# Byte offsets of TensorE's operands: g in rows of 2064 bytes, g_lo 8 bytes further, and h, p and a at multiples of 64

## The chip, the cores and the metric

One core of a Trainium2 chip runs the whole program. The metric is device time of one execution in microseconds. The clock of TensorE is told below as the granted clock of the trace, as a share of 2.4 GHz.

## What is computed

The input x has 32 images of 32 x 32 positions with 256 channels. Each image goes through a group normalisation, a one-head attention over its 1024 positions and an output projection, and x is added:

```python
h = group_norm(x)                      # 32 groups of 8 channels
q, k, v = h @ Wq + bq, h @ Wk + bk, h @ Wv + bv
attn = softmax((q @ k.T) * 256 ** -0.5)        # 1024 x 1024 for each image
out = x + (attn @ v) @ Wo + bo
```

## The kernel before

**Number format.** Every large product is made of three products in float32r: each factor is split into a rounded part (hi) and the rest (lo), and hi x hi, hi x lo and lo x hi are summed in PSUM.

**Folded weights.** At the start, Wq and Wk are folded into one matrix a, and Wv and Wo into one matrix vo, so that an image needs the projection g = a.h + g_bias, the scores g.h, the projection v = h.vo, and the attention p.v.

**Stages of TensorE.** The order is written out by hand. Each image b has five kinds of stage, and a matmul here is one instruction with its own weight load of 128 x 128:

- `project_g` (G): 24 matmuls with 512 columns each. Stationary is a, moving is h. The result goes through ScalarE (`g_part`, writes g_hi) and VectorE (`g_rest`, writes g_lo).
- `scores` (S): twice 48 matmuls with 512 columns, for the halves c = 0 and 1 of the queries. Stationary is h (columns m x 128), moving is g (block kk, c). For each m they come as (h_hi, g_hi), (h_hi, g_lo), (h_lo, g_hi) for kk = 0 and then for kk = 1.
- `project_v` (V): 48 matmuls with 256 columns. Stationary is h, moving is vo.
- `attend` (A): twice 96 matmuls with 258, 256 and 258 columns in turn. Stationary is p_hi or p_lo, moving is v_hi (rows of 258 columns) or v_lo (rows of 256).

The sequence for one image in the steady loop is `scores(b, 0)`, `attend(b - 1, 1)`, `project_v(b)`, `scores(b, 1)`, `attend(b, 0)`, `project_g(b + 1)`. Over 32 images this makes 768 G, 3072 S, 1536 V and 6144 A matmuls, 11520 in all. ScalarE and VectorE do the softmax and the splits beside it; SyncE and GpSimd issue the transfers.

**Where the tensors lie.** `sb(name, shape)` allocates a tensor in SBUF behind the one before it, at the next multiple of 32 bytes. So the order of the calls and their sizes set every start address. In the built program the tensors that TensorE reads start at these bytes of each partition:

| tensor | bytes before | past a multiple of 64 | bytes after | past a multiple of 64 |
|---|---|---|---|---|
| a_hi, a_lo | 17568, 19616 | 32 | 17536, 19584 | 0 |
| vo_hi, vo_lo | 21664, 23712 | 32 | 79200, 81248 | 32 |
| h_hi, h_lo | 35008, 43200 | 0 | 29824, 38016 | 0 |
| g_hi, g_lo | 51392, 59584 | 0 | 46208, 54464 | 0 (g_lo is read from 8 on) |
| v_hi, v_lo | 67776, 76032 | 0 | 62720, 70976 | 0 |
| p_hi (c = 0, 1) | 118368, 134752 | 32 | 83328, 99712 | 0 |
| p_lo (c = 0, 1) | 151136, 167520 | 32 | 116096, 132480 | 0 |

Inside the tensors, weight blocks and the blocks of h, p, a, vo and v_lo lie multiples of 512 bytes apart, so they keep the tensor's offset. A row of v_hi has 258 columns, 1032 bytes, so row m starts 8m bytes past a multiple of 64.

Of the kernel before, what the change touches and what calls it, by code (L numbers as in the profile page):

```python
# [31 lines left out]
F32 = mybir.dt.float32  # L32
F32R = mybir.dt.float32r
ALU = mybir.AluOpType
ACT = mybir.ActivationFunctionType
AX_X = mybir.AxisListType.X

P = 128
# [4 lines left out]
def attention_kernel(nc, x, x_turned, wq, bq, wk, bk, wv, bv, wo, bo, out):  # L43
    B, H, W, C = x.shape
    N = H * W
    T = N // P
    K = C // P
    CH = 2
    Q = N // CH
# [6 lines left out]
    NG = SQ // GC  # L56
    QB = Q // SQ
    SB = 4
    VC = C + 2
    SCALE = float(C) ** -0.5  # L60


# [3 lines left out]
    with ExitStack() as ctx:  # L66
        def sb(name, shape, dt=F32):
            return ctx.enter_context(nc.sbuf_tensor(name, shape, dt))
# [4 lines left out]
        def banks(name, n):  # L73
            return [ctx.enter_context(nc.psum_tensor(f"{name}{i}", [P, 512], F32)) for i in range(n)]
# [4 lines left out]
        ps_s = banks("ps_s", SB)  # L79
        ps_o = banks("ps_o", TQ)  # L80
        ps_g = [ps_o[0], ps_o[1], ps_s[2], ps_s[3]]
# [3 lines left out]

        ident = sb("ident", [P, P])
        ones = sb("ones", [P, P])
        minus_half = sb("minus_half", [P, NG])
        a_hi = sb("a_hi", [P, K, C], F32R)
        a_lo = sb("a_lo", [P, K, C], F32R)  # L90
        vo_hi = sb("vo_hi", [P, K, C], F32R)
        vo_lo = sb("vo_lo", [P, K, C], F32R)
        g_bias = sb("g_bias", [P, K])
        out_bias = sb("out_bias", [P, C])


        x_t = sb("x_t", [P, K, N])
        h_hi = sb("h_hi", [P, K, N], F32R)
        h_lo = sb("h_lo", [P, K, N], F32R)
        g_hi = sb("g_hi", [P, K, N], F32R)  # L100
        g_lo = sb("g_lo", [P, K, N], F32R)
        v_hi = sb("v_hi", [P, T, VC], F32R)
        v_lo = sb("v_lo", [P, T, C], F32R)
        bn_parts = sb("bn_parts", [P, K, 2, 6])


# [10 lines left out]


        s_buf = [sb(f"s_buf{c}", [P, T, Q]) for c in range(CH)]
        p_hi = [sb(f"p_hi{c}", [P, T, Q], F32R) for c in range(CH)]  # L120
        p_lo = [sb(f"p_lo{c}", [P, T, Q], F32R) for c in range(CH)]
        top2 = sb("top2", [P, 2, Q])
        top_turned = sb("top_turned", [P, Q])
        part_max = sb("part_max", [P, QB])
# [67 lines left out]
        def after(eng, semaphore, value):  # L192

            if not isinstance(value, int) or value > 0:
                eng.wait_ge(semaphore, value)
# [54 lines left out]
        def _(pool):  # L250
# [4 lines left out]
            pool.memset(v_hi[:, :, C:C + 1].bitcast(F32), 1.0).then_inc(const_step, 1)  # L255
            pool.memset(v_hi[:, :, C + 1:VC].bitcast(F32), 0.0).then_inc(const_step, 1)
            pool.wait_ge(const_step, 6)
# [28 lines left out]
        def _(act):  # L286
# [12 lines left out]
            def g_part(b, i):  # L299
                act.wait_ge(g_ps, b * 4 + (i + 1))  # L300
                c, k = i // 2, i % 2
                nc.scalar.activation(g_hi[:, k, c * Q:(c + 1) * Q], ps_g[i][:], ACT.Identity,
                                     bias=g_bias[:, k:k + 1]).then_inc(g_hi_done, 1)

            def v_part(b, i):
# [10 lines left out]
            def exponentials_hi(b, c, i):  # L316

                rows = slice(i * PIECE, (i + 1) * PIECE)
                if i == 0:
                    after(act, o_ps, b * 8 + (4 * c + 4 - 8))  # L320
                act.wait_ge(diff_done, b * 8 + (4 * c + i + 1))
                nc.scalar.activation(p_hi[c][:, rows, :], s_buf[c][:, rows, :], ACT.Exp,  # L322
                                     scale=SCALE).then_inc(p_hi_done, 1)

            def exponentials(b, c, i):

                piece = s_buf[c][:, i * PIECE:(i + 1) * PIECE, :]
                nc.scalar.activation(piece, piece, ACT.Exp, scale=SCALE).then_inc(p_done, 1)  # L328

# [20 lines left out]
            for i in range(4):  # L350
                g_part(0, i)
# [36 lines left out]
            def body(b, first, last):  # L388

                scores_out(b, 0, 0)  # L390
                if not first:
                    last_exponentials(b - 1, 1)
                for m in range(1, T):
                    scores_out(b, 0, m)
                if first:
                    first_softmax()
                else:
                    softmax_beside(b, 0, lambda i: v_part(b, i))
                    scores_out(b, 1, 0)
                    last_exponentials(b, 0)  # L400
                    for m in range(1, T):
                        scores_out(b, 1, m)
                if not last:
                    h_parts(b + 1)
                softmax_beside(b, 1, nothing if last else (lambda i: g_part(b + 1, i)))
# [6 lines left out]
        def _(dve):  # L412
# [69 lines left out]

            def g_rest(b, i):
                c, k = i // 2, i % 2
                cols = slice(c * Q, (c + 1) * Q)
                dve.wait_ge(g_hi_done, b * 4 + (i + 1))
                nc.vector.scalar_tensor_tensor(out=g_lo[:, k, cols], in0=ps_g[i][:], scalar=g_bias[:, k:k + 1],
                                               in1=g_hi[:, k, cols].bitcast(F32), op0=ALU.add,
                                               op1=ALU.subtract).then_inc(g_lo_done, 1)

            def v_rest(b, i):
# [100 lines left out]
            for i in range(4):  # L592
                g_rest(0, i)
# [59 lines left out]
            def body(b, first, last):  # L653
# [26 lines left out]
                if not first and not last:  # L680
                    normalise(b + 1)
                maxima(b, 1, 3)
                maxima(b, 1, 4)
                softmax_beside(b, 1, lambda j: finish(b, 0, j), nothing if last else (lambda k: h_rest(b + 1, k)),
                               nothing if last else (lambda i: g_rest(b + 1, i)), nothing, nothing)

            images(dve, body)
# [5 lines left out]
        def _(pe):  # L693
            def product(ps, pairs, sem_done, start=True, stop=True):

                for n, (stationary, moving) in enumerate(pairs):
                    last = nc.tensor.matmul(ps, stationary, moving, start=start and n == 0,  # L697
                                            stop=stop and n == len(pairs) - 1)
                if sem_done is not None:
                    last.then_inc(sem_done, 1)  # L700
# [54 lines left out]
            def scores(b, c, m):  # L755

                if m == 0:
                    pe.wait_ge(g_lo_done, b * 4 + (2 * c + 2))
                if m in (2, 3):

                    pe.wait_ge(v_lo_done if c else g_lo_done, b * 4 + (m + 1))
                after(pe, s_out, b * 16 + (8 * c + m + 1 - SB))
                rows, cols = slice(m * P, (m + 1) * P), slice(c * Q, (c + 1) * Q)
                product(ps_s[(8 * c + m) % SB][:], [(h[:, kk, rows], g[:, kk, cols]) for kk in range(K)
                                                    for h, g in ((h_hi, g_hi), (h_hi, g_lo), (h_lo, g_hi))], s_ps)

            def attend(b, c, j):
# [7 lines left out]
                for m in range(T):  # L775
                    if j == 0 and m % PIECE == 0:
                        pe.wait_ge(p_lo_done, b * 8 + (4 * c + m // PIECE + 1))
                    nc.tensor.matmul(ps[:, 0:VC], p_hi[c][:, m, cols], v_hi[:, m, :], start=m == 0, stop=False)  # L778
                    nc.tensor.matmul(ps[:, 0:C], p_hi[c][:, m, cols], v_lo[:, m, :], start=False, stop=False)  # L779
                    last = nc.tensor.matmul(ps[:, 0:VC], p_lo[c][:, m, cols], v_hi[:, m, :], start=False,  # L780
                                            stop=m == T - 1)
# [25 lines left out]
            def body(b, first, last):  # L807
                for m in range(T):
                    scores(b, 0, m)
                if not first:  # L810
                    for j in range(TQ):
                        attend(b - 1, 1, j)
                project_v(b)
                for m in range(T):
                    scores(b, 1, m)
                for j in range(TQ):
                    attend(b, 0, j)
                if not last:
                    project_g(b + 1)
# [35 lines left out]
```

## Time and profile before

| | us |
|---|---|
| median of 2 runs | 1836.41 (1836.28 to 1836.55) |
| the profiled execution | 1837.21 |
| its span, first to last instruction | 1835.5 |
| TensorE busy | 1815.1 |
| TensorE's weight loads busy | 1655.1 |
| VectorE busy | 1662.1 |
| ScalarE busy | 985.9 |
| mean granted TensorE clock | 0.994 |

The span is what the trace covers; the profiled execution has 1.7 us outside it. A matmul's busy time in the trace is longer than the distance from its start to the next one's start, since matmuls overlap in the array. So the distance of two starts, here called the pitch, is what a matmul costs on a TensorE that never rests, and the timeline is the view to read it from.

### The profile page before, as it was taken

What the parts mean: (1) busy time and instruction counts of PE and PEld (TensorE: products, weight loads), DVE (VectorE), ACT (ScalarE), POOL (GpSimd) and SP (SyncE); (2) the same over time, 40 slices, a digit from 0 to 9 for tenths busy, and PEclk for the clock granted to TensorE, in tenths of its full rate; (3) what the DMA queues carried; (4) which work ended last, traced back from release to release, by engine and by line L of the source; (5) the groups of instructions that cost most, each with busy time, mean ns of one, the idle gap of its engine ahead of it and who ended that gap; (6) DMA issues with size and microseconds to landing.
All of it is one profiled execution on the core that took longest, in us unless ns stands there. A gap on an engine that the chain in (4) does not pass through costs nothing.

```text
span 1835.5 us, 32744 instructions
## 1 busy us (share of the span) xinstructions
PE 1815.1 (99%) x11586; PEld 1655.1 (90%) x11586; DVE 1662.1 (91%) x2922; ACT 985.9 (54%) x1352; POOL 91.1 (5%) x107
## 2 busy tenths in 40 slices
PE   8999999999999999999999999999999999999997
PEld 7899999899898999998998989999989989899996
DVE  7899999999999999999999999999999999999985
ACT  4564654654645646546555456465465554564652
POOL 0000000000000000000000000000000000000000
PEclk9999999999999999999999999999999999999998
DMA  3221222221222212222212222122222122221211
GB/s 115 58 69 34 46 69 57 69 62 18 69 57 69 69 34 46 69 57 69 61 19 69 57 69 69 30 50 69 57 69 59 21 69 57 69 69 27 53 23 24
DMA packets 29296, 101.92 MB, mean 56 GB/s; under 512 B 3681, under 2 KB 4706, under 8 KB 29282
## 3 DMA queue, kind: packets, MB, share of 16 engines
q0 software_dynamic: 9216, 33.56, 11.6%
q1 hardware_dynamic: 20066, 68.17, 11.6%
q8 instruction: 9, 0.15, 0.0%
q14 instruction: 5, 0.04, 0.0%
HBM read 68.16 MB, written 67.11 MB: 74 GB/s over the span
## 4 chain that ended last, share of the span: by engine, by line
PE 98%; DVE 1%; DMA 0%; issue 0%; SPq 0%; POOLq 0%; ACT 0%; DVEq 0%
PE ps_s L697 48%; PE ps_o L778 13%; PE ps_o L780 13%; PE ps_o L779 13%; PE ps_o L697 10%; DMA s_buf<-in_L_conv_Wk_dram 0%; DVE p_lo L545 0%; DVE s_buf L537 0%; DVE v_lo L493 0%; PE ps_o L709 0%; DVE top L507 0%; DVE query_max L524 0%; PE ps_s L709 0%; POOLq L66 0%; SPq L213 0%
## 5 line engine op out<-in xcount | busy, mean ns | idle before, releaser
L778 PE MATMUL ps_o<-v_hi,p_hi 128*128 128x258 f32 x2048 | 580.3, 283 | 3.2 <-DVE p_lo L545 3.2
L780 PE MATMUL ps_o<-v_hi,p_lo 128*128 128x258 f32 x2048 | 580.6, 284 | 0.0
L779 PE MATMUL ps_o<-v_lo,p_hi 128*128 128x256 f32 x2048 | 578.1, 282 | 0.0
L322 ACT ACTIVATE p_hi<-s_buf 128x1024 fp32r<-128x1024 f32 x256 | 272.0, 1062 | 525.8 <-DVE s_buf L537 525.8
L697 PE MATMUL ps_s<-g_hi,h_hi 128*128 128x512 f32 x1024 | 398.6, 389 | 1.5 <-DVE v_lo L493 1.5
L697 PE MATMUL ps_s<-g_hi,h_lo 128*128 128x512 f32 x1024 | 399.5, 390 | 0.0
L697 PE MATMUL ps_s<-g_lo,h_hi 128*128 128x512 f32 x1024 | 398.9, 390 | 0.0
L778 PEld LDWEIGHTS ps_o<-v_hi,p_hi 128*128 128x128 f32 x2048 | 389.0, 190 | 6.1 <-issue 2.2
L779 PEld LDWEIGHTS ps_o<-v_lo,p_hi 128*128 128x128 f32 x2048 | 388.6, 190 | 3.0
L780 PEld LDWEIGHTS ps_o<-v_hi,p_lo 128*128 128x128 f32 x2048 | 388.5, 190 | 0.0
L314 ACT ACTIVATE s_buf<-ps_s 128x512 f32<-128x512 f32 x512 | 292.9, 606 | 167.9 <-PE ps_s L697 164.0
L545 DVE TENSOR_TENSOR p_lo<-s_buf,p_hi 128x1024 fp32r<-128x1024 f32 x256 | 306.6, 1218 | 32.0 <-ACT s_buf L328 32.0
L537 DVE TENSOR_TENSOR s_buf<-s_buf,row_max 128x1024 f32<-128x1024 f32 x256 | 306.6, 1218 | 1.1
L328 ACT ACTIVATE s_buf<-s_buf 128x1024 f32<-128x1024 f32 x256 | 270.9, 1058 | 0.0
L697 PEld LDWEIGHTS ps_s<-g_hi,h_hi 128*128 128x128 f32 x1024 | 192.4, 188 | 41.4 <-DVE v_lo L493 2.0
L697 PEld LDWEIGHTS ps_s<-g_hi,h_lo 128*128 128x128 f32 x1024 | 192.2, 188 | 40.2
L697 PEld LDWEIGHTS ps_s<-g_lo,h_hi 128*128 128x128 f32 x1024 | 192.2, 188 | 39.5
L507 DVE TENSOR_TENSOR top<-top,s_buf 128x512 f32<-128x512 f32 (+1 forms) x192 | 166.8, 869 | 46.9 <-ACT s_buf L314 35.6
L557 DVE SCALAR_TENSOR_TENSOR o_buf<-ps_o,rden,out_bias 128x256 f32<-128x256 f32 x256 | 123.9, 484 | 14.7
L265 POOL DMA_DIRECT2D out_dram<-o_buf x64 | 57.0, 891 | 1429.0 <-DVE o_buf L557 1358.9
L307 ACT ACTIVATE v_hi<-ps_o 128x512 fp32r<-128x512 f32 x64 | 38.3, 599 | 107.0 <-PE ps_o L697 107.0
L507 DVE TENSOR_TENSOR top<-s_buf 128x1024 f32<-128x1024 f32 x64 | 78.3, 1223 | 8.2 <-ACT s_buf L314 8.2
(89 smaller groups left out, 2202.9 us busy)
## 6 DMA issues: line engine op xcount, KB each, us to landing
x_t<-in_x_turned_dram SPq DMA_DIRECT2D x64, 512.0 KB, 3.7
out_dram<-in_x_dram SPq DMA_DIRECT2D x64, 512.0 KB, 7.5
out_dram<-o_buf POOLq DMA_DIRECT2D x64, 512.0 KB, 5.5
s_buf<-in_L_conv_Wq_dram SPq DMA_DIRECT2D x1, 256.0 KB, 5.0
s_buf<-in_L_conv_Wk_dram SPq DMA_DIRECT2D x1, 256.0 KB, 6.2
s_buf<-in_L_conv_Wv_dram SPq DMA_DIRECT2D x1, 256.0 KB, 5.5
s_buf<-in_L_conv_Wo_dram SPq DMA_DIRECT2D x1, 256.0 KB, 6.6
s_buf<-in_L_conv_bq_dram SPq DMA_DIRECT2D x1, 1.0 KB, 6.3
```

The lines of the kernel that those rows point to most:

```text
L265: pool.dma_start(out_v[b, :, c * TQ:(c + 1) * TQ, :], o_buf[c][:], accum_op=ALU.add).then_inc(stored[c], 16)
L314: nc.scalar.activation(s_buf[c][:, m, :], ps_s[(8 * c + m) % SB][:], ACT.Copy).then_inc(s_out, 1)
L322: nc.scalar.activation(p_hi[c][:, rows, :], s_buf[c][:, rows, :], ACT.Exp, scale=SCALE).then_inc(p_hi_done, 1)
L328: nc.scalar.activation(piece, piece, ACT.Exp, scale=SCALE).then_inc(p_done, 1)
L507: nc.vector.tensor_tensor(to, left, right, ALU.max).then_inc(top_step, 1)
L537: nc.vector.tensor_tensor(piece, piece, row_max[:].unsqueeze(1).broadcast_to([P, PIECE, Q]), ALU.subtract).then_inc(diff_done, 1)
L545: nc.vector.tensor_tensor(p_lo[c][:, rows, :], s_buf[c][:, rows, :], p_hi[c][:, rows, :].bitcast(F32), ALU.subtract).then_inc(p_lo_done, 1)
L557: nc.vector.scalar_tensor_tensor(out=o_buf[c][:, j, :], in0=ps_o[j][:, 0:C], scalar=rden[:, t:t + 1], in1=out_bias[:], op0=ALU.mult, op1=A ...
L697: last = nc.tensor.matmul(ps, stationary, moving, start=start and n == 0, stop=stop and n == len(pairs) - 1)
L778: nc.tensor.matmul(ps[:, 0:VC], p_hi[c][:, m, cols], v_hi[:, m, :], start=m == 0, stop=False)
L779: nc.tensor.matmul(ps[:, 0:C], p_hi[c][:, m, cols], v_lo[:, m, :], start=False, stop=False)
L780: last = nc.tensor.matmul(ps[:, 0:VC], p_lo[c][:, m, cols], v_hi[:, m, :], start=False, stop=m == T - 1)
```

## The change

The tensors are allocated in another order, and g gets a gap of 4 columns behind each block of 512. Of a block with index 2k + c, g_hi then starts 16 (2k + c) bytes past a multiple of 64: 0 and 32 for c = 0, 16 and 48 for c = 1. g_lo starts 8 bytes behind each: 8 and 40 for c = 0, 24 and 56 for c = 1. The small tensors `shift` and `shift_back` are never used; they put vo at 32 past a multiple of 64 and p at 0. Against their stationary operand (as "moving minus stationary", modulo 64) the moving operands stand like this:

| stage | before | after |
|---|---|---|
| G (h against a) | 32 | 0 |
| S (g against h) | 0 | 0, 8, 0, 32, 40, 32 for c = 0; 16, 24, 16, 48, 56, 48 for c = 1 |
| V (vo against h) | 32 | 32 |
| A (v_hi, v_lo, v_hi against p) | 8m + 32, 32, 8m + 32 | 8m, 0, 8m |

No instruction is added, removed or moved on any engine: each engine's list has the same instructions with the same shapes in the same order, and the waits are the same.

```diff
+    GROW = Q + 4
...
-        minus_half = sb("minus_half", [P, NG])
+
         a_hi = sb("a_hi", [P, K, C], F32R)
         a_lo = sb("a_lo", [P, K, C], F32R)
-        vo_hi = sb("vo_hi", [P, K, C], F32R)
-        vo_lo = sb("vo_lo", [P, K, C], F32R)
-        g_bias = sb("g_bias", [P, K])
-        out_bias = sb("out_bias", [P, C])
-
-
         x_t = sb("x_t", [P, K, N])
         h_hi = sb("h_hi", [P, K, N], F32R)
         h_lo = sb("h_lo", [P, K, N], F32R)
-        g_hi = sb("g_hi", [P, K, N], F32R)
-        g_lo = sb("g_lo", [P, K, N], F32R)
+
+        g_rows = [sb("g_hi", [P, K, CH, GROW], F32R), sb("g_lo", [P, K, CH, GROW], F32R)]
+        g_hi, g_lo = g_rows[0][:, :, :, 0:Q], g_rows[1][:, :, :, 2:2 + Q]
         v_hi = sb("v_hi", [P, T, VC], F32R)
         v_lo = sb("v_lo", [P, T, C], F32R)
+        sb("shift", [P, 8])
+        vo_hi = sb("vo_hi", [P, K, C], F32R)
+        vo_lo = sb("vo_lo", [P, K, C], F32R)
+        sb("shift_back", [P, 8])
+        p_hi = [sb(f"p_hi{c}", [P, T, Q], F32R) for c in range(CH)]
+        p_lo = [sb(f"p_lo{c}", [P, T, Q], F32R) for c in range(CH)]
+
+        minus_half = sb("minus_half", [P, NG])
+        g_bias = sb("g_bias", [P, K])
+        out_bias = sb("out_bias", [P, C])
...
-        p_hi = [sb(f"p_hi{c}", [P, T, Q], F32R) for c in range(CH)]
-        p_lo = [sb(f"p_lo{c}", [P, T, Q], F32R) for c in range(CH)]
...
-                product(ps_s[(8 * c + m) % SB][:], [(h[:, kk, rows], g[:, kk, cols]) for kk in range(K)
+                product(ps_s[(8 * c + m) % SB][:], [(h[:, kk, rows], g[:, kk, c, :]) for kk in range(K)
```

`g_part` and `g_rest` index g in the same new way.

## Rows read from the trace of the kernel before

**Rows 1.** The page: busy time of each engine, and the chain that ended last

```profile
PE 1815.1 (99%) x11586; PEld 1655.1 (90%) x11586; DVE 1662.1 (91%) x2922; ACT 985.9 (54%) x1352; POOL 91.1 (5%) x107
...
PE 98%; DVE 1%; DMA 0%; issue 0%; SPq 0%; POOLq 0%; ACT 0%; DVEq 0%
```

**Rows 2.** The waits of TensorE: us in total, times, longest

```profile
PE ps_o L778 <- DVE p_lo L545: 3.2, 2, 2.0
PE ps_o L697 <- issue: 2.1, 1, 2.1
PE ps_o L786 <- POOL ident L258: 2.0, 1, 2.0
PE ps_o L709 <- DMA s_buf<-in_L_conv_Wk_dram: 1.9, 1, 1.9
PE ps_s L697 <- DVE v_lo L493: 1.5, 1, 1.5
```

**Rows 3.** Timeline, TensorE, scores of image 3, c = 1: start, duration (us)

```profile
213.97 0.40 PE L697 MATMUL ps_s<-g_hi,h_hi 128*128 128x512 f32 x1
...
214.67 0.39 PE L697 MATMUL ps_s<-g_hi,h_hi 128*128 128x512 f32 x1
214.90 0.39 PE L697 MATMUL ps_s<-g_lo,h_hi 128*128 128x512 f32 x1
...
216.05 0.39 PE L697 MATMUL ps_s<-g_hi,h_hi 128*128 128x512 f32 x1
...
224.44 0.39 PE L697 MATMUL ps_s<-g_lo,h_hi 128*128 128x512 f32 x1
```

**Rows 4.** The same view, the next image's project_g and the start of its scores

```profile
236.42 0.40 PE L697 MATMUL ps_o<-h_hi,a_hi 128*128 128x512 f32 x1
...
239.21 0.40 PE L697 MATMUL ps_s<-h_hi,a_hi 128*128 128x512 f32 x1
...
242.01 0.39 PE L697 MATMUL ps_s<-g_hi,h_hi 128*128 128x512 f32 x1
```

**Rows 5.** The same view at project_g of image 1, behind a wait

```profile
66.41 0.47 PE L697 MATMUL ps_o<-h_hi,a_hi 128*128 128x512 f32 x1 [2.09 <-issue]
...
67.29 0.63 PE L697 MATMUL ps_o<-h_hi,a_hi 128*128 128x512 f32 x1
...
69.85 0.63 PE L697 MATMUL ps_o<-h_hi,a_hi 128*128 128x512 f32 x1
```

**Rows 6.** Stretches: us, busy by engine (instructions), granted clock, DMA share, GB/s

```profile
core 0: us, PE busy (x) PEld busy (x) DVE busy (x) ACT busy (x) POOL busy (x), PEclk, DMA share, GB/s
...
67.30:70.20 2.90, 2.90 (x8) 2.33 (x7) 2.87 (x5) 2.58 (x3) 0.00 (x0) 0.50 0.94 332
...
200.00:220.00 20.00, 20.00 (x146) 18.94 (x145) 18.43 (x35) 11.28 (x16) 0.86 (x1) 1.00 0.17 26
```

**Rows 7.** Timeline, TensorE: the first matmul of project_v of image 3

```profile
208.28 0.29 PE L697 MATMUL ps_o<-vo_hi,h_hi 128*128 128x256 f32 x1
```

**Rows 8.** Timeline, TensorE: first and last matmul of attend(3, 0)

```profile
224.90 0.28 PE L778 MATMUL ps_o<-v_hi,p_hi 128*128 128x258 f32 x1
...
236.29 0.28 PE L780 MATMUL ps_o<-v_hi,p_lo 128*128 128x258 f32 x1
```

More of the change, by code:

```diff
@@ L301, in g_part @@
                 c, k = i // 2, i % 2
-                nc.scalar.activation(g_hi[:, k, c * Q:(c + 1) * Q], ps_g[i][:], ACT.Identity,
+                nc.scalar.activation(g_hi[:, k, c, :], ps_g[i][:], ACT.Identity,
                                      bias=g_bias[:, k:k + 1]).then_inc(g_hi_done, 1)
@@ L484, in g_rest @@
                 c, k = i // 2, i % 2
-                cols = slice(c * Q, (c + 1) * Q)
                 dve.wait_ge(g_hi_done, b * 4 + (i + 1))
-                nc.vector.scalar_tensor_tensor(out=g_lo[:, k, cols], in0=ps_g[i][:], scalar=g_bias[:, k:k + 1],
-                                               in1=g_hi[:, k, cols].bitcast(F32), op0=ALU.add,
+                nc.vector.scalar_tensor_tensor(out=g_lo[:, k, c, :], in0=ps_g[i][:], scalar=g_bias[:, k:k + 1],
+                                               in1=g_hi[:, k, c, :].bitcast(F32), op0=ALU.add,
                                                op1=ALU.subtract).then_inc(g_lo_done, 1)
@@ L762, in scores @@
                 after(pe, s_out, b * 16 + (8 * c + m + 1 - SB))
-                rows, cols = slice(m * P, (m + 1) * P), slice(c * Q, (c + 1) * Q)
-                product(ps_s[(8 * c + m) % SB][:], [(h[:, kk, rows], g[:, kk, cols]) for kk in range(K)
+                rows = slice(m * P, (m + 1) * P)
+                product(ps_s[(8 * c + m) % SB][:], [(h[:, kk, rows], g[:, kk, c, :]) for kk in range(K)
                                                     for h, g in ((h_hi, g_hi), (h_hi, g_lo), (h_lo, g_hi))], s_ps)
```

## The prediction

> **What bounds the kernel now.** I read the page first, for which engine the end hangs on. TensorE is busy 1815.1 of 1835.5 us and makes 98% of the chain that ended last [rows 1]. Its waits for others sum to 10.7 us in six places [rows 2], so nothing but the pace of its own 11520 matmuls is left to shorten. VectorE is next with 1662.1 us [rows 1], 173 us below the span; in 20 us of the steady loop it is busy 18.43 us [rows 6]. A TensorE faster by a per cent or two would not run into it often.
>
> Then I read the pace in the timeline, by the pitch from one start to the next. In each stage I compare it with the bare columns at the granted clock of 1.00 [rows 6], which is 2.4 GHz: 512 columns take 213.3 ns, 256 take 106.7.
>
> - S, settled: from 216.05 to 224.44 there are 37 pitches, 8.39 us, 226.8 ns each: 13.4 over the columns [rows 3].
> - S, unsettled: after project_v the first nine pitches, 213.97 to 216.05, take 2.08 us, 231.1 each, and one of them (214.67 to 214.90) takes 0.23 [rows 3]. The same operands' offsets thus give two paces.
> - G: the last twelve pitches, 239.21 to 242.01, take 2.80 us, 233.3 each: 20.0 over the columns. The first twelve, 236.42 to 239.21, take 2.79 [rows 4].
> - V: 48 pitches from 208.28 to 213.97 take 5.69 us, 118.5 each: 11.9 over [rows 3, 7].
> - A: 96 pitches from 224.90 to 236.42 take 11.52 us, 120.0 each. Two in three have 258 columns, so the columns are 107.2 and the excess is 12.8 [rows 4, 8].
>
> The excess over the columns is 3072 x 13.5 + 768 x 20 + 1536 x 11.9 + 6144 x 12.8 ns = 41 + 15 + 18 + 79 = 153 us. That is all that any placement of operands can win.
>
> Two more things speak of where the excess comes from. Image 1's project_g runs at a granted clock of 0.50, 1.2 GHz [rows 6], behind a wait of 2.09 us; its pitch is then (69.85 - 67.29) / 6 = 426.7 ns, exactly 512 columns at 1.2 GHz [rows 5]. The excess is gone when the array asks for columns half as fast, so it is not a fixed cost of an instruction; it is the feeding of the operands. And G and S are the same shape, the same type and the same count of weights. What differs is that g lies at 0 against h (modulo 64 bytes), while h lies at 32 against a. G costs 6.5 ns more for each matmul. That is the only pair in this trace from which a price of the offset can be read, and it is a correlation in two stages.
>
> A rule of the Trainium skill speaks against any effect at all. SBUF — State Buffer, in the section on two separate sides, and TensorE: Matmul & The Clock Gate, in the steps of a matmul, say that TensorE has one read port for the moving operand and another for the weights, so that a load does not take bandwidth from a running matmul. By that rule the offsets change nothing. The second page's section on the back-to-back gap gives 512 columns 2.5 ns over the bare columns; this trace shows 13.4 and 20.0, so something that this rule leaves out is at work here.
>
> **The change part by part.** It moves no instruction, so each term is a count times a change of pitch. The 10.7 us of waits stay; they are before first results and at the last image.
>
> *a to offset 0 (G).* h against a goes from 32 to 0, what S has now. If the pitch goes from 233.3 to S's 226.8, 24 matmuls x 6.5 ns x 31 images (one has ten at the low clock) = 4.8 us. If each project_g first passes through nine unsettled pitches at 231.1, as S does behind project_v, 9 x 4.3 x 31 = 1.2 us of it are lost. The ends are 0 and -5; I take **-4 us**, nearer to the settled row, since scores behind project_g settle at once.
>
> *g spread over eight offsets (S).* This is the largest unknown: 3072 pitches, 3.1 us for each ns. The nearest rows are at the same shape: 226.8 (all at 0), 233.3 (G, all at 32), 231.1 (at 0, unsettled). Half of the hi blocks of c = 0 are now at 32 and half at 0; c = 1 has 16 and 48, the lo blocks 8 to 56, and for those no row exists. If all of S ran at 231.1, the term is +13 us; at G's pace +20 us. On the good side the shortest pitch in the row is about 224 ns, which gives -8 us, and V's excess of 11.9 ns on 512 columns would be 225.2, -5 us. If the spread does remove most of the collision, a pitch of 220 gives -21 us. One more hint for the sizes: the settled pitch 226.8 is close to 17 x 13.33 ns, that is to 17 times 16 ticks of 1.2 GHz. If the six matmuls of one m settle together on such a multiple, S moves in steps of 13.3 / 6 = 2.2 ns, 6.8 us each. The nearest rows on both sides (-8 and +13) leave a middle slightly above nothing, and the spread's aim slightly below. I take **0** and keep -21 to +20.
>
> *p to offset 0 (A).* v_hi against p takes the same eight offsets as before in another order of m, so 4096 of 6144 pitches have no direction. v_lo against p goes from 32 to 0 in 2048. If the price of 32 goes with the columns, it is 3.3 ns for 256 of them and the term is -6.7 us. But V has all its operands at 32 and yet the lowest excess of all stages, 11.9 against A's 12.8, so at 256 columns the price of 32 may be nothing. I take half, **-3 us**. As bounds I take 1.5 ns both ways for all 6144, somewhat over the 0.9 by which the two rows of this width differ: -9 to +9.
>
> *vo and the rest.* V keeps its 32: nothing. VectorE and ScalarE read and write g_lo, s_buf and p at new addresses. Their instructions run beside TensorE, and its waits for them are three, 4.7 us in all [rows 2]; nothing, and if VectorE had to pay 1% of its 1662 us, 17 us, the gap of 173 us would hide nearly all.
>
> The sum is -4 + 0 - 3 = -7 us on the profiled execution's 1837.2, that is 1830.2. The median lies 0.8 below that execution, so the forecast is **1830 us**.
>
> **The rivals.**
>
> *S loses its settled pace (slower).* S has the lowest excess per column of this trace, 13.4 ns on 512 against A's 12.8 on 257, perhaps just because all its moving operands stand at one offset and each matmul meets the next in the same phase. With six different offsets in six matmuls, it would run at the unsettled 231.1: +13 us, with the other terms at -4 and 0: 1845. It decides for slower from the point where S's mean pitch passes 229.1 (2.3 x 3.07 = 7 us). For it: the two paces in rows 3. Against it: G's moving operands share one offset too and have no such pace, so sharing alone doesn't make S fast.
>
> *The spread works (clearly faster).* Operands at different offsets don't meet in the same place of the memory again and again. S at 220 ns gives -21, A -3 and G -4: 1808; a half of it 1818. For it: the excess is large, 41 us in S alone, and vanishes at the low clock. Against it: S at one offset is already better than G.
>
> *Nothing answers to offsets (the rule of the two ports).* The difference of G and S then has another cause, such as the position in the loop or the store of the result in other banks. Every pitch stays, 1836 us. For it: only one pair speaks for a price of the offset. Against it: the second half of G writes to banks that S writes to as well, and still has 233.3 [rows 4].
>
> **How the numbers follow.** The forecast (1824 to 1836, small gains in G and A) gets 0.40. The clear gain (below 1824) gets 0.28, the loss of the pace in S (above 1838) 0.22, and no answer (about 1836) 0.10. The range takes in the terms' bounds without their extremes at once: -4 - 21 - 6 gives 1805, and -2 + 15 + 3 gives 1852; I set **1804 to 1852**. Two per cent, about what a measurement of this kernel can tell from no change, is 37 us. Faster by more needs nearly the whole excess of S or -21 in S with 12 or more in A: 0.07. Slower by more needs +20 in S and over 17 in A: 0.03. Within it: 0.90.
>
> **What would show it.** Right: project_g of image 4 takes 5.45 us instead of 5.59; the 37 last pitches of scores stay within 225 to 229 ns; attend takes 11.45 to 11.5 us for 96. Wrong: scores at 231 ns and over, or at 222 and below; they alone move the total by 10 us and more. A changed list of TensorE's waits, or a G that stays at 233 with a at 0, would show that the offset against the stationary operand is not the quantity that counts.

## The result and the profile after

The changed kernel takes 1854.93 us (1854.12 to 1855.75, 2 runs) against 1836.41: a ratio of 1.0101, 95% interval 1.0083 to 1.012. It is slower by 1%, which is small but clear of the interval. The forecast of 1830 (1804 to 1852) was wrong: the sign, and by 3 us the range too. Of all executions in this study two ran with a low mean clock, one of the kernel before (2286.75 us at 0.729) and one of h1 below (3001.99 us at 0.564); they are in no ratio.

The profiled execution has 1854.12 us and a span of 1852.4, 16.9 more than before. The first two lines of the page answer to [rows 1]:

```profile
PE 1831.8 (99%) x11586; PEld 1659.0 (90%) x11586; DVE 1663.7 (90%) x2922; ACT 984.7 (53%) x1352; POOL 91.1 (5%) x107
...
PE 98%; DVE 1%; issue 0%; DMA 0%; POOL 0%; POOLq 0%; ACT 0%; SPq 0%; DVEq 0%
```

TensorE has 16.7 us more of busy time with the same 11586 instructions; VectorE has 1.6 more and ScalarE 1.2 less, and the chain is the same. So nobody makes TensorE wait: its matmuls have become slower. Its waits, which answer to [rows 2], sum to 11.0 us against 10.7:

```profile
PE ps_o L781 <- DVE p_lo L548: 3.2, 2, 2.0
PE ps_o L789 <- POOL ident L262: 2.0, 1, 2.0
PE ps_o L700 <- issue: 1.9, 1, 1.9
PE ps_s L700 <- DVE v_lo L496: 1.5, 1, 1.5
PE ps_o L712 <- DMA s_buf<-in_L_conv_Wk_dram: 1.1, 1, 1.1
PE ps_o L700 <- DVE o_buf L587: 1.0, 1, 1.0
PE ps_s L712 <- DMA s_buf<-in_L_conv_Wo_dram: 0.3, 1, 0.3
```

Which stage is slower shows in the timeline of TensorE at the stage borders of one image (start, duration): scores c = 0, attend, project_v, scores c = 1, attend, project_g with its second half, and the next scores.

```profile
186.46 0.39 PE L700 MATMUL ps_s<-g_hi,h_hi 128*128 128x512 f32 x1
...
197.74 0.28 PE L781 MATMUL ps_o<-v_hi,p_hi 128*128 128x258 f32 x1
...
209.27 0.28 PE L700 MATMUL ps_o<-vo_hi,h_hi 128*128 128x256 f32 x1
...
214.96 0.39 PE L700 MATMUL ps_s<-g_hi,h_hi 128*128 128x512 f32 x1
...
226.11 0.28 PE L781 MATMUL ps_o<-v_hi,p_hi 128*128 128x258 f32 x1
...
237.65 0.39 PE L700 MATMUL ps_o<-h_hi,a_hi 128*128 128x512 f32 x1
...
240.41 0.39 PE L700 MATMUL ps_s<-h_hi,a_hi 128*128 128x512 f32 x1
...
243.13 0.39 PE L700 MATMUL ps_s<-g_hi,h_hi 128*128 128x512 f32 x1
```

| stage of an image | before, us | after, us | all images |
|---|---|---|---|
| scores c = 0 (48 pitches) | 10.89 (48 x 226.8, [rows 3]) | 11.28 | +12.6 |
| scores c = 1 | 10.93 [rows 3, 8] | 11.15 | +6.8 |
| project_v | 5.69 [rows 3, 7] | 5.69 | +0.1 |
| attend, twice | 11.51 each [rows 4, 8] | 11.53 and 11.54 | +1.5 |
| project_g | 5.59 [rows 4] | 5.48 | -3.3 |

The last column sums the differences of all 32 images. Together they are +17.6. The span has 16.9, because the first project_g also starts 0.7 us earlier, at 16.92 instead of 17.62 us.

### The profile page after: what moved, and what is told of

Read it like the earlier page. It is cut to its first block, busy times and chain, and to the rows that moved or that the text cites. A ratio compares the mean times of both kernels' runs of the same rounds, so it can differ in the third digit from the quotient of the medians.

```text
span 1852.4 us, 32744 instructions
## 1 busy us (share of the span) xinstructions
PE 1831.8 (99%) x11586; PEld 1659.0 (90%) x11586; DVE 1663.7 (90%) x2922; ACT 984.7 (53%) x1352; POOL 91.1 (5%) x107
## 4 chain that ended last, share of the span: by engine, by line
PE 98%; DVE 1%; issue 0%; DMA 0%; POOL 0%; POOLq 0%; ACT 0%; SPq 0%; DVEq 0%
PE ps_s L700 48%; PE ps_o L783 13%; PE ps_o L781 13%; PE ps_o L782 13%; PE ps_o L700 10%; DMA x_t<-in_x_turned_dram 0%; DVE p_lo L548 0%; DVE s_buf L540 0%; DVE x_t L473 0%; DVE bn_parts L422 0%; DVE v_lo L496 0%; DVE top L510 0%; DVE h_lo L479 0%; POOL group_stats L274 0%; DVE query_max L527 0%
## 5 line engine op out<-in xcount | busy, mean ns | idle before, releaser
L700 PE MATMUL ps_s<-g_hi,h_lo 128*128 128x512 f32 x1024 | 409.0, 399 | 0.0
L700 PE MATMUL ps_s<-g_lo,h_hi 128*128 128x512 f32 x1024 | 405.0, 395 | 0.0
```

## Experiments

A settled pitch below is the mean of the pitches once they repeat themselves: over the last 36 of a scores half, the last 12 of project_g, pitches 17 to 40 of project_v or the last three quarters of attend, without the last pitch before the next stage. It is read from the timeline of the steady loop; the first image and, for project_g, image 1 are left out, and what they do is told where it matters. Most kernels ran once only, and their totals are given against the kernel before on the same chip. Totals also move by up to 2 us for two reasons that have nothing to do with the layout: in 11 of the 20 traces project_g of image 1 falls to a granted clock of 0.50 as in [rows 5, 6], which makes it 1.2 us longer, and the first project_g starts between 16.7 and 18.0 us. So the stages decide, not the totals.

**First round: undo parts of the change to g.** All four keep the changed kernel's distances of project_g and attend, and vo's place modulo 64. Modulo 256 vo moves, and project_v takes 5.76 us instead of 5.69 in all four, 2 us over the run. g has rows of 2112 bytes (of 2048 in e3), and a table says how many columns each block is shifted:

```diff
-    GROW = Q + 4
+    GROW = Q + 16
+    G_SHIFT = (((0, 8), (4, 12)), ((0, 8), (4, 12)))   # e1: hi, lo; c; k
+    G_SHIFT = (((0, 0), (0, 0)), ((2, 2), (2, 2)))     # e2
+    G_SHIFT = (((0, 0), (0, 0)), ((0, 0), (0, 0)))     # e3, with GROW = Q
+    G_SHIFT = (((8, 8), (4, 4)), ((8, 8), (4, 4)))     # e4
```

> The changed kernel without the 8 bytes between g_lo and g_hi: both start at 16 (2k + c) bytes past a multiple of 64 (rows of 2112 bytes). Scores pitch in the changed kernel: 235 ns for c = 0, 232 for c = 1; before: 226.7. Theory A, the 8 bytes cost it (a moving operand that starts in the middle of 16 bytes): both halves back to 227 or a little over, total about 1835. Theory B, the spread of offsets over the matmuls that follow each other costs it, since the settled pace of before is lost: nearly unchanged, 231 to 235, total 1850 to 1855. Theory C, only the distance of a moving operand from its own stationary operand counts (0 cheap, 32 dear): c = 0, half at 0 and half at 32, at 230; c = 1, at 16 and 48, unknown; total 1840 to 1850.

> All blocks of g_hi at 0 past a multiple of 64, all of g_lo at 8 (rows of 2112 bytes); the rest as in the changed kernel. Theory A (the 8 bytes): scores at 232 to 235 in both halves, total 1850 to 1855. Theory B (the spread): two offsets that alternate are a small spread, 228 to 231. Theory C (distance from the stationary): g_lo's third at a distance of 8 may cost something, g_hi's two thirds stay at 227; 227 to 230. Both halves should be equal in every theory.

> The changed kernel with g in rows of 2048 bytes and all blocks at 0 past a multiple of 64, as before; a, p and h stay at 0 and vo at 32. All theories of the scores: pitch 226.7 again. project_g keeps the changed kernel's gain (settles at 227), attend keeps its own pitch of the changed kernel, so the total is the before time less 3.3 us of project_g and plus 1.5 of attend: 1834 to 1836. If scores don't return to 227, the cost is in something else that moved, such as h's or g's absolute place.

> No spread within a half: all blocks of g for c = 0 at 32 past a multiple of 64, all for c = 1 at 16 (hi and lo alike, rows of 2112 bytes). Theory C (the distance counts): c = 0 at G's pace of before, 233; c = 1 between 227 and 233 or above. Theory B (the spread costs, a shared offset lets the matmuls settle): both halves at about 227. Theory A: both at 227, since no block starts in the middle of 16 bytes.

Measured (before: 1838.09 on this chip): e1 1846.48, e2 1848.16, e3 1836.25, e4 1852.74 us. In e3, with g back at 0, the scores are back too. Timeline, TensorE, its two halves of scores:

```profile
184.75 0.39 PE L705 MATMUL ps_s<-g_hi,h_hi 128*128 128x512 f32 x1
...
195.63 0.29 PE L786 MATMUL ps_o<-v_hi,p_hi 128*128 128x258 f32 x1
...
212.93 0.39 PE L705 MATMUL ps_s<-g_hi,h_hi 128*128 128x512 f32 x1
...
223.85 0.29 PE L786 MATMUL ps_o<-v_hi,p_hi 128*128 128x258 f32 x1
```

10.88 and 10.92 us are the halves of before. Settled pitches are 226.7 in e3. As means of all 48 they are 230.9 and 231.1 in e1, 232.5 and 230.1 in e2, 234.3 and 231.9 in e4. So the 8 bytes are not the cause alone (e1 has none and is slow), and neither is a difference between hi and lo (e1 and e4 have none). The two halves of e2 differ, though they are alike modulo 64, which no theory had. The rows of 2112 bytes move each block by 64 more: e2's g_hi blocks stand 0 and 128 bytes from h for c = 0 and 64 and 192 for c = 1. So 64 is too small a modulus. This also makes e1 and e4 less pure than meant: e4's "32" was 32 and 160, its "16" was 80 and 208.

**Second round: one distance for a stage, modulo 256.** From here a helper places each tensor, and the blocks of g lie 2048 bytes apart in a tensor for each half. Only the settings change between kernels.

```diff
+        AT = dict(a=192, h=0, v=0, v_lo=64, vo=0, p=160)   # bytes past a multiple of 256
+        G_AT = ...                                          # the same for each block of g
+        def at(past, name, shape, dt=F32R):
+            gap = (past - end[0]) % 256
+            if gap:
+                sb(f"gap_{name}", [P, gap // 4])
...
+        h_hi = at(AT["h"], "h_hi", [P, K, N])
```

> Every stage at one distance of moving minus stationary operand, counted modulo 256 bytes now, since the run with g_lo 8 bytes further had different paces in its two halves though both were alike modulo 64. Blocks of g no longer differ modulo 256 within a half. Scores c = 0 at 32, c = 1 at 16, project_g at 64, project_v at 0, attend (v_hi of row 0 against p) at 96 as in the kernel before. Theory distance modulo 64: c = 0 at about 233 as project_g had at 32, c = 1 at about 232 as in the run with 16, project_g at 64 like 0, so 227 when settled. Theory distance modulo 256: project_g at 64 may differ from 227. Theory spread: both scores at 227, since each half has one offset.

> Scores c = 0 at a distance of 64, c = 1 at 128, project_g at 128, project_v at 32, attend at 64. Theory distance modulo 64: scores settle at 227 in both halves and project_g too. Theory distance modulo 128 or 256: one or both of the halves at 230 to 235. Theory spread: 227 in both.

> Scores c = 0 with all of g at 8, c = 1 with g_hi at 0 and g_lo at 8; project_g at 192, project_v at 128, attend at 0. Theory 8 bytes cost by themselves (a start in the middle of 16 bytes): c = 0 at 235 or more, c = 1 at 230. Theory distance: c = 0 between 227 and 235 and c = 1 between it and 227. Theory spread: c = 0 at 227, c = 1 above it.

> Scores c = 0 with the kk = 0 blocks at 0 and the kk = 1 blocks at 32 (a spread in two steps), c = 1 all at 224; project_g at 224, project_v at 160, attend at 160. Theory distance: c = 0 halfway between 227 and 233, 230; c = 1 and project_g alike, near 233. Theory spread: c = 0 above 230, c = 1 at 227.

Measured (before: 1836.23): f1 1850.76, f2 1841.31, f3 1847.29, f4 1849.56 us. f1's halves, with all of g at 32 and at 16 (rows of equal names are merged in pairs here, and the start is the first's):

```profile
186.06 0.62 PE L715 MATMUL ps_s<-g,h_hi 128*128 128x512 f32 x2
...
197.25 0.29 PE L796 MATMUL ps_o<-v_hi,p_hi 128*128 128x258 f32 x1
...
214.50 0.40 PE L715 MATMUL ps_s<-g,h_hi 128*128 128x512 f32 x1
...
225.62 0.28 PE L796 MATMUL ps_o<-v_hi,p_hi 128*128 128x258 f32 x1
```

11.19 and 11.12 us: the scores at 32 settle at 233.3 ns, exactly what project_g had at 32 in the kernel before [rows 4]. The agreement goes down to the order of the single pitches. Both repeat four of 235.0, 233.3, 234.2 and 230.8 ns. Likewise scores and project_g at 64 both repeat 225.8, 229.2, 231.7 and scores and project_g at 224 both repeat 231.7, 235.0. Those are two stages with other tensors and with other work on VectorE and the DMA engines beside them. In f2 the scores at 64 and at 128, both 0 modulo 64, settle at 228.9 and 232.4, so the distance modulo 64 is out as a rule.

A mixture of distances is not the average of its parts. f3's half with g_hi at 0 and g_lo at 8 settles at 233.3, above both 226.7 (all at 0) and 232.2 (all at 8), and 5 ns above their average weighted by count. f4's half with its kk = 0 blocks at 0 and its kk = 1 blocks at 32 settles at 231.1, 1 ns above its average. By the table below, e1's and e4's mixed halves lie within 1.3 ns of their averages, above or below. Nor does a difference between hi and lo always cost: e2's second half, with g_hi at 64 and 192 and g_lo 8 bytes further, settles at 230.0, below the 231.1 that 64 and 192 would average.

**Third round: is it a rule one can build with?**

> Each stage at the cheapest distance (moving minus stationary, modulo 256 bytes) of the runs so far: scores 0, project_g 0, project_v 32, attend 0 (v_lo then at 64). Theory distance: the paces of the stages add up from other runs, whatever stands together: scores 226.7 once settled, project_g 227 once settled, project_v 116.7, attend 119.3. Against before that is -3 us (project_g), -2.6 (1536 x 1.7 ns), -3.7 (6144 x 0.6 ns): about 1827. Rival: the paces were chance phases of each kernel, and don't return in another layout; then 1832 to 1842.

> The absolute place tested: h and all that is placed against it moved by 96 bytes; project_g stays at 0, project_v at 32, attend at 0. Scores at two distances not yet tried, 96 (c = 0) and 160 (c = 1). Theory distance: project_g settles at 227, project_v at 116.7, attend at 119.3 as in the unmoved kernel. If the absolute place counts, these three differ. For the scores: the distances tried so far gave 227 (0), 229 (64), 232 to 233.5 (8, 16, 32, 128, 192, 224); these two will lie between 227 and 235.

> Scores at 48 (c = 0) and 80 (c = 1), project_g at 96, project_v at 64, attend at 32. Theory distance: project_g at 96 settles in exactly the rhythm of the scores at 96 in the run before. The scores at 227 to 235; a distance below 227 would be a new best. Theory absolute place: no such agreement.

> Scores at 208 (c = 0) and 4 (c = 1), project_g at 160, project_v at 192, attend with v_hi and v_lo both at 0. Theory distance: project_g at 160 has the rhythm of the scores at 160; a distance of only 4 bytes from the best one tells how sharp it is: if whole lines of 16 bytes count, 4 settles at 227 like 0; if each byte counts, it lies above 229. Attend: v_lo at 0 instead of 64 changes 119.3 by up to 1 ns either way.

h1 takes 1826.62 us (ratio 0.995, 95% interval 0.9936 to 0.9963), where 1827 was expected. The borders of its stages:

```profile
185.44 0.39 PE L715 MATMUL ps_s<-g,h_hi 128*128 128x512 f32 x1
...
196.32 0.28 PE L796 MATMUL ps_o<-v_hi,p_hi 128*128 128x258 f32 x1
...
207.78 0.28 PE L715 MATMUL ps_o<-vo_hi,h_hi 128*128 128x256 f32 x1
...
213.38 0.40 PE L715 MATMUL ps_s<-g,h_hi 128*128 128x512 f32 x1
```

Scores 10.88, attend 11.46 instead of 11.51, project_v 5.60 instead of 5.69. h2 (1843.79 us) has h, a and vo 96 bytes further on modulo 256. It keeps project_g's 226.7 and project_v's 116.7, so the absolute place does not set the settled pace of these two. (Attend's v and p were not moved against 256, so its 119.3 says nothing on this.) Its scores at 96 settle in the same three pitches (231.7, 237.5, 230.8) as h3's project_g at 96. h3 takes 1838.3 and h4 1853.72 us. h4's half at 4 bytes is the dearest of all, 237.3 ns: the cheap place is sharp. Its attend, which differs from h1's only in v_lo at 0 instead of 64, settles at 120.0 against 119.4.

All scores, project_g and project_v stages that had one distance, in ns of settled pitch (those of the fourth round are in it):

| distance | 512 columns | 256 columns (project_v) |
|---|---|---|
| 0 | 226.7 | 120.0 |
| 4, 8, 16 | 237.3, 232.2, 231.6 | |
| 32 | 233.3 | 116.7 |
| 48 | 233.3 | |
| 64 | 228.9 | 113.3 or 117.8 |
| 80, 96, 112 | 231.1, 233.3, 231.1 | 120.0 at 96 |
| 128 | 232.4 | 118.6 |
| 144, 160, 176 | 233.3, 234.2, 233.3 | 120.0 at 160 |
| 192 | 233.3 | 113.3 or 117.8 |
| 208, 224, 240 | 234.6, 233.3, 233.3 | 118.3 at 224 |

**Fourth round: g alone, and attend.** k1, k2, k4 and l2 give v_hi rows of 1280 bytes, so that its distance to p no longer marches by 8 bytes a row.

```diff
-        v_hi = at(AT["v"], "v_hi", [P, T, VC])
+        v_hi = at(AT["v"], "v_hi", [P, T, C + 64])[:, :, 0:VC]
```

k3 is the kernel before with nothing but g's new rows:

```diff
-        g_hi = sb("g_hi", [P, K, N], F32R)
-        g_lo = sb("g_lo", [P, K, N], F32R)
+        g_rows = [sb("g_hi", [P, K, CH, GROW], F32R), sb("g_lo", [P, K, CH, GROW], F32R)]
+        g_hi, g_lo = g_rows[0][:, :, :, 0:Q], g_rows[1][:, :, :, 2:2 + Q]
+        sb("gap", [P, 32])
```

> The kernel before with only g's new rows: blocks 2064 bytes apart, g_lo 8 further, and a gap behind g_lo so that v, p and all others keep their places modulo 256. Theory distance: scores as in the changed kernel, 235.5 (c = 0) and 232.2 (c = 1), which is +19 to +20 us; project_g, project_v and attend settle as in the kernel before. Total 1855 to 1857. Rival (h's or p's new place had a part in the loss): less than +17 us.

> Rows of v_hi 1280 bytes apart (258 columns used), so that every moving operand of attend stands at one distance from p: 64 for v_hi and v_lo. project_v at 64 too, scores and project_g at 0. Theory distance: attend gets project_v's pace at 64, 113.3 ns for 256 columns and 114.2 for 258, so 113.9 in the mean instead of 119.3; 6144 x 5.4 ns = 33 us, and project_v 1536 x 3.3 = 5 us less than at 32. From 1826.6 that gives 1788 to 1790, if VectorE, busy 1663 us, keeps up. Rival (attend pays for its 258 columns or its stationary p, whatever the distance): attend stays at 119 to 120, total 1821.

> The same rows of v_hi, but attend at distance 0 for v_hi and v_lo; project_v at 192, scores at 112 (c = 0) and 144 (c = 1), project_g at 0. Theory distance: attend gets project_v's pace at 0, 120.0 for 256 columns, so 120 to 121; project_v at 192 is 113.3 as before; scores above 227 in both halves. Rival: attend at the same pace as in the run with 64.

> Rows of v_hi 1280 bytes apart, attend at distance 192 for v_hi and v_lo; project_v at 64, scores at 240 (c = 0) and 176 (c = 1), project_g at 0. Theory distance: attend at project_v's pace at 192, 113.3 for 256 columns, 113.9 in the mean; scores at 227 to 235. Rival (attend pays whatever the distance): 119 to 120.

k3 takes 1852.95 us against 1835.15. Its scores:

```profile
185.62 0.39 PE L699 MATMUL ps_s<-g_hi,h_hi 128*128 128x512 f32 x1
...
196.89 0.28 PE L780 MATMUL ps_o<-v_hi,p_hi 128*128 128x258 f32 x1
...
214.09 0.39 PE L699 MATMUL ps_s<-g_hi,h_hi 128*128 128x512 f32 x1
...
225.23 0.28 PE L780 MATMUL ps_o<-v_hi,p_hi 128*128 128x258 f32 x1
```

11.27 and 11.14 us are the changed kernel's 11.28 and 11.15, settled pitches 235.5 and 232.2 in both, in the same order of single pitches; everything else has the paces of before. So g's rows make the whole loss in the scores, (0.38 + 0.21) x 32 = 19 us. The total is a little below the forecast one, at least in part since this run's project_g of image 1 kept the full clock, as this stretch shows beside [rows 6]:

```profile
67.00:70.00 3.00, 3.00 (x15) 2.41 (x14) 2.96 (x6) 2.75 (x4) 0.00 (x0) 1.00 0.86 302
```

k1 takes 1820.74 us (ratio 0.9917, 95% interval 0.9903 to 0.993), k2 1844.49, k4 1845.35. Attend of k1, and then its project_v:

```profile
223.64 0.28 PE L796 MATMUL ps_o<-v_hi,p_hi 128*128 128x258 f32 x1
...
235.01 0.39 PE L715 MATMUL ps_o<-h_hi,a_hi 128*128 128x512 f32 x1
```

```profile
207.08 0.28 PE L715 MATMUL ps_o<-vo_hi,h_hi 128*128 128x256 f32 x1
...
212.74 0.39 PE L715 MATMUL ps_s<-g,h_hi 128*128 128x512 f32 x1
```

Attend has 11.37 us, settled 118.2 ns: it does follow the distance (120.0 at 0 in k2, 118.9 at 192 in k4), but it is far from the 113.9 that was expected for 64 and 192, and the 1788 us with it. The total is the 1821 us that the rival gave. project_v at 64 has 5.66 us and 117.8 ns in k1 and k4, where h3 had 113.3, and at 192 it has 117.8 in k2, where h4 had 113.3. The last two runs looked into that.

> The kernel with each stage at the cheapest distance (v_hi rows of 1032 bytes, attend at 0), with project_v at 64 instead of 32. Theory two paces at one distance, chosen by how the stage is entered: project_v is entered from the attend with rows of 1032 bytes, as in the two kernels that had 113.3; it may be 113.3 (total 1821 to 1822) or 117.7 (total 1828), and no third. Theory one pace for a distance, with v's rows of 1280 bytes as the cause of 117.7: 113.3 for sure.

> Rows of v_hi 1280 bytes apart, attend at a distance of 32 for v_hi and v_lo, project_v at 64, scores and project_g at 0. Theory distance: attend near project_v's pace at 32, 116.7 for 256 columns, so 117.3 in the mean with the 258; against 118.2 at 64 that is 6 us less, total 1815 to 1817 with project_v at 117.7, 1808 to 1810 with it at 113.3. Rival (what attend pays does not follow project_v's distances): 118 to 120, total 1820 to 1832.

l1 takes 1825.61 us, its project_v settles at 117.8. Timeline of project_v at the same distance of 64, first h3, then l1:

```profile
208.12 0.28 PE L715 MATMUL ps_o<-vo_hi,h_hi 128*128 128x256 f32 x1
...
213.56 0.39 PE L715 MATMUL ps_s<-g,h_hi 128*128 128x512 f32 x1
```

```profile
205.53 0.28 PE L715 MATMUL ps_o<-vo_hi,h_hi 128*128 128x256 f32 x1
...
211.18 0.40 PE L715 MATMUL ps_s<-g,h_hi 128*128 128x512 f32 x1
```

5.44 against 5.65 us, and l1 has v's rows of 1032 bytes like h3, so those rows are not the reason. At 256 columns one distance has at least two settled paces, and no third was seen in the seven kernels at 64 or 192.

The trace of h3 holds both paces at once. In its first image project_v follows scores and not attend. Its first matmul there, and that of the scores behind it:

```profile
33.67 0.28 PE L715 MATMUL ps_o<-vo_hi,h_hi 128*128 128x256 f32 x1
...
39.32 0.39 PE L715 MATMUL ps_s<-g,h_hi 128*128 128x512 f32 x1
```

That is 5.65 us, settled at 117.8, at a granted clock of 1.00; the other 31 images have 5.44 and 113.3. The addresses are the same, so the layout alone doesn't choose the pace: something in how the stage is entered, or in what only the first image has, does. It isn't simply the stage before it, since h4's first project_v, at 192, also follows scores and settles at 113.3. Stages of 512 columns do it too: the first scores of f2 at 64 settle at 233.3 where all later ones have 228.9, the first of h4 at 208 at 230.0 instead of 234.6, and those of image 1 in f3 at 8 at 233.3 instead of 232.2. What the choice hangs on was not found.

l2 is the best kernel of this study: 1818.61 us, ratio 0.9907, 95% interval 0.9891 to 0.9924. Its attend at 32:

```profile
222.93 0.28 PE L796 MATMUL ps_o<-v_hi,p_hi 128*128 128x258 f32 x1
...
234.25 0.40 PE L715 MATMUL ps_o<-h_hi,a_hi 128*128 128x512 f32 x1
```

11.32 us, 117.8 ns settled, 12 us less than before over the 64 halves. That lies between the distance theory's 117.3 and the rival's 118, and the total lies between their ranges too, so l2 decides for neither. Attend is within 0.6 ns of project_v's paces, corrected for its 258 columns, at 0, 32, 64 and 192, if the slower of the two is taken at 64 and 192. Distance moves attend's pace; that project_v's table foretells it is not shown.

## Why the prediction was wrong

- **What bounds the kernel: right.** TensorE's own pace was all that changed, and the waits stayed (11.0 against 10.7 us). That the pace answers to where the operands lie was right as well: 512 columns settle at 226.7 to 237.3 ns by the distance of the two operands. The Trainium skill (SBUF — State Buffer, two separate sides) gives TensorE two independent read ports. The prediction drew from it that offsets change nothing, and these runs contradict that. But the 153 us were not all to be won: no settled pitch of any run is below 226.7 for 512 columns or 113.3 for 256, which is 17/16 of the bare columns in both cases. Whether placement can touch that last sixteenth is open, and so is what it comes from. That the excess vanishes at 1.2 GHz doesn't by itself show that it is the feeding of operands, as the prediction put it.
- **a to offset 0: right.** -3.3 us against -4. The nine unsettled pitches came as priced: the first twelve of project_g take 2.76 us, the other twelve 2.72, which is 226.7 each.
- **g spread over eight offsets: the step that failed.** The term was taken as 0, with -21 to +20 around it; it measured +19.4, the outer end (k3, with this change alone, has +19.0). With this term at 0 the measured others, -3.3 and +1.5, would have given 1835. Two things were wrong in it. The middle was taken between the pace of 0 and better ones, though the two distances that the trace had (0 at 226.8 and 32 at 233.3) already said that leaving 0 costs, and no row showed a distance below it; none of the 17 other distances that the runs tried is cheaper. And the mixture was thought of as an average, while c = 0 settles at 235.5, above the 233.3 of its dearer g_hi block. A mixture of hi and lo can cost more than its parts, as f3 shows (233.3 from parts of 226.7 and 232.2). How much of the 235.5 is mixture and how much the g_lo distances is open: 72, 88, 104 and 120 were never run alone, and of the distances that are no multiple of 16 only 4 and 8 were. The changed g_lo moreover stood at 72, 104, 88 and 120 from h, not at 8, 40, 24 and 56, because g_hi's 8256 bytes push it by 64; a table modulo 64 hides that.
- **p to offset 0: wrong in sign, small.** -3 was taken, +1.5 measured. The step read offsets modulo 64. Modulo 256, v_lo against p went from 160 to 192, not from 32 to 0, and v_hi's rows went from 96 + 8m to 128 + 8m, so they did not keep "the same eight offsets". The step also scaled a price from 512 columns down to 256, where the order is another one: 0 has 120.0 and 32 has 116.7. Its counter-hint, project_v's low excess "at 32", was in fact at 224. No run moved v_lo or v_hi alone from these places, so which of the two cost the 1.5 us is open.
- **The rivals.** The loss of the settled pace in S came nearest, at 1845 us and a chance of 0.22, 10 us below the measured time. It took the unsettled 231.1 as the price; the measured means are 235.0 for c = 0 (11.28 / 48) and 232.3 for c = 1. Its reason was not enough either, as its own "against it" said: f1 shares one offset in each half and has 233.3 and 231.6. The distance 0 makes S fast. Nor was a settled pace lost: the changed kernel's scores settle too, in a dearer cycle.
- **The steps of 2.2 ns.** Half as large a step fits. The pitches of one settled cycle sum to a multiple of 6.67 ns, 16 columns at 2.4 GHz, wherever a cycle could be made out: 226.7 is 34 of them, four pitches of 233.3 are 140, the six of the changed kernel's c = 0 are 212 and the six of c = 1 are 209. The last is no multiple of 13.3 ns.

## What to carry to other kernels

When TensorE is never idle, compare the pitch of its matmuls with the bare columns. If the excess differs between stages of one shape, look at the byte distance of the moving and the stationary operand modulo 256, in the built program's addresses and not in the source; a pad of some bytes between two tensors is then worth a sweep, each stage and each column count by itself. Here it won 1% (1836 to 1819 us). Put all of a stage's operands at the one cheapest distance instead of spreading them, and judge a layout by the pitches of its stages: the total mixes them with a clock that falls in one run and not in the next.

## What the runs showed of the hardware

- The pitch of a float32r matmul with its own weight load depends on (moving - stationary start) modulo 256 bytes: 226.7 to 237.3 ns for 512 columns, 113.3 to 120.0 for 256. f2's project_g at 128 and its scores at 384 (modulo 512) repeat the same seven pitches, and h1's two halves at 0 and 256 both have 226.7, so 256 is enough. 64 and 128 are not: 0, 64, 128 and 192 have 226.7, 228.9, 232.4 and 233.3. Moving both operands by 96 bytes leaves the settled pace as it was.
- The weight load of a matmul starts one pitch before it, beside the matmul before (in the kernel before, the load for the matmul at 200.14 us starts at 200.02). All stationary operands of a stage start at one place modulo 256 in every run, so the runs can't tell whether the distance to a matmul's own weights counts or that to the next one's.
- A stage of one distance with 512 or 256 columns takes up to 13 pitches to settle and then repeats the same few in every image of the loop, to 1 to 3 ns. Other work doesn't show in them: at one distance scores and project_g repeat the same pitches, though in the kernel before the DMA share is 0.06 beside settled scores and 0.93 beside project_g. In the first two images a stage can settle at another pace. At 1.2 GHz the excess is nothing at all, 426.7 ns for 512 columns [rows 5].
- The Trainium skill (SBUF — State Buffer, Door 1: The DMA port swizzle) speaks of lines of 16 bytes in SBUF and of a penalty for each crossing. The dearest distance, 4 bytes (237.3), starts inside such a line, but 8 bytes does too and costs 232.2, less than 32 with 233.3; so crossings alone don't order the table.
- Which memory is met by both operands at the same time, and why 0 is cheap at 512 columns and dear at 256, was not settled.
